# The last feed-forward of a decoder layer on one core: kept feature-major, with slots of 512 tokens

## The chip, the cores and the metric

The kernel runs on 1 core of one Trainium2 chip, as one program of six stages. The metric is the device time of one execution in microseconds. Engines are called as in the profile: PE (TensorE, with PEld for its weight loads), DVE (VectorE), ACT (ScalarE), POOL (GpSimd) and SP (the queue that issues DMAs).

## What is computed

A decoder layer over 4 sequences of 1024 tokens with 512 features: attention, a cross block with its own feed-forward, and last a quantised feed-forward, which is the only part that the change touches. Cut to that part:

```python
def act_quant(x):
    scale = 127.0 / clip(max(abs(x), axis=-1, keepdims=True), 1e-05)
    return clip(round(x * scale), -128, 127) / scale

x = layernorm(x)                         # 4 x 1024 x 512
h = einsum('bsd,hd->bsh', act_quant(x), weight_quant(w1))      # 512 -> 2048
h = depthwise_conv1d(h, conv_w, conv_b)  # 3 taps along the tokens, per feature
h = silu(h)
out = x_in + einsum('bsd,hd->bsh', act_quant(h), weight_quant(w2))   # 2048 -> 512
```

The convolution runs along the tokens of one feature. The quantisation of h needs, for each token, the largest absolute value over its 2048 features, and multiplies all of the token's features by one scale.

## The kernel before, in words

`quantised_ffn` (lines 2226 to 2550) is the last stage. The stage ahead has left the quantised x transposed in DRAM (`xq_parts`), with one scale factor per token (`x_units`); the weights w1 and w2 lie in DRAM as bf16 integers. Every engine has an instruction list of its own, written out by hand, and engines are tied by semaphores alone: `wait_ge` holds the engine's whole list until a count is reached. The order in each list is therefore what sets the order of the work.

For each of the 4 sequences (`body`) there are two halves.

- *Convolution half*, features on the partitions, 16 blocks (HB) of 128 features by 1024 tokens (T). PE makes a block in two PSUM banks of 512 tokens (L2424). DVE multiplies each bank by the token factors into `y` (`dequantise`, L2527). ACT makes the centre tap with the bias (L2465) and the right tap (L2468); DVE makes the centre tap of every fourth block instead (L2534) and adds the left tap for all (`add_left`, L2541); POOL adds the right tap (L2375); ACT applies SiLU into `h` (L2450), two blocks behind. y has two buffers, conv three.
- *Token half*, 8 tiles of 128 tokens. PE turns a tile of h, 16 transposes of 128 x 128 in fp32 (`turn_h`, L2394), so that tokens stand on the partitions. DVE takes the largest absolute value per token from PSUM (L2503) and makes the scale in five small steps (L2508 to L2497). ACT scales and adds 1.5 * 2^23, which rounds (L2456); POOL subtracts it again and writes bf16 (L2367). PE turns the tile back, 16 transposes in bf16 (`turn_hq`, L2403), ACT copies it out of PSUM (L2483), and PE multiplies by w2, 16 products (L2411). DVE scales the result and adds the residual (`finish`, L2517), SP stores it.

The token half of one sequence and the convolution half of the next use the same PSUM banks (`big`), so they follow one another.

SP's queue issues the loads (L2318, L2320, L2327, L2328, L2336) and the stores (L2324). At the start PE waits for both weights before its first product.

## Time and profile before

| | us |
|---|---|
| median of 3 runs (3616.22 to 3622.75) | 3618.28 |
| the profiled execution, its time | 3615.1 |
| the profiled execution, its span (first to last instruction) | 3613.4 |
| first issue of the last stage (SP L2318) | 3094.76 |
| first DVE pass of the last stage (L2527) | 3118.49 |

Busy over the whole span: PE 88%, PEld 64%, DVE 65%, ACT 51%, POOL 30%. These shares are means over six stages with different limits, and the last stage is about one seventh of the span. A line of the profile gives, for a group of equal instructions, how many there are (x64), the sum of their time, the mean of one in ns, and how long the engine stood idle just ahead of them and for whom. A timeline row gives start, length and, in brackets, the idle time ahead with its releaser. L numbers are lines of the kernel.

### The profile page before, as it was taken

Reading aid. Unit: us, or ns where it says so; the run is one execution under the profiler, and the core shown is the slowest. Engines: PE = TensorE matmul, PEld = TensorE weight load, DVE = VectorE, ACT = ScalarE, POOL = GpSimd, SP = SyncE. Lnnn points to the kernel's source line nnn. Section 1 sums busy time; section 2 is a strip of 40 time slices with the busy share of each in tenths; the row PEclk is TensorE's granted clock in tenths of the full one; section 3 lists DMA queues with packets and bytes.
Section 4 is the critical chain, followed back from the end, with each engine's and each line's share of the span. In section 5 each row is a group of like instructions: output and inputs, shape, how many; then the busy total and the mean of one; then the engine's idle time right before and its main releaser. Section 6 shows DMA issues by size and latency. Waiting matters only on the chain. (4 is left out here: it accounts for less than half of the span.)

```text
span 3613.4 us, 55879 instructions
## 1 busy us (share of the span) xinstructions
PE 3183.6 (88%) x19218; PEld 2307.8 (64%) x19218; DVE 2336.2 (65%) x4146; ACT 1842.0 (51%) x2979; POOL 1079.9 (30%) x829
## 2 busy tenths in 40 slices
PE   6998999999999999599996998599999998376687
PEld 5776666666666666377774777488878886143244
DVE  5563888888888888445644888444444445567766
ACT  3331888888888888322222222222222221467676
POOL 2343213112211311242322454211111110356555
PEclk9999999999999999799997999799999999688998
DMA  6775113212212221555536343321111101320111
GB/s 212 243 248 164 56 56 90 61 55 80 71 58 64 82 63 56 182 194 187 200 128 199 117 146 102 127 69 31 37 34 41 42 30 41 94 65 18 47 47 42
DMA packets 239599, 350.47 MB, mean 97 GB/s; under 512 B 31792, under 2 KB 129104, under 8 KB 239440
## 3 DMA queue, kind: packets, MB, share of 16 engines
q1 hardware_dynamic: 208784, 291.46, 25.2%
q0 software_dynamic: 8640, 31.77, 2.6%
q10 hardware_dynamic: 22016, 25.17, 2.0%
q8 instruction: 93, 1.52, 0.2%
q14 instruction: 66, 0.54, 0.1%
HBM read 210.68 MB, written 137.64 MB: 96 GB/s over the span
## 5 line engine op out<-in xcount | busy, mean ns | idle before, releaser
L863 DVE CUSTOM_DVE_ANT_0 attend_scores<-attend_scores,attend_bias_table 128x1024 f32<-128x1024 f32 x512 | 630.4, 1231 | 163.4 <-PE attend_scores L717 157.0
L790 ACT ACTIVATE attend_probs<-attend_scores,attend_neg_max 128x1024 f32<-128x1024 f32 x512 | 571.0, 1115 | 136.6 <-DVE attend_neg_max L863 126.7
L729 PE MATMUL attend_turned<-attend_ident,attend_probs 128*128 128x128 f32 x4096 | 556.5, 275 | 11.4 <-DVE attend_probsT L871 11.2
L729 PEld LDWEIGHTS attend_turned<-attend_ident,attend_probs 128*128 128x128 f32 x4096 | 471.9, 140 | 121.1 <-DVE attend_probsT L871 28.1
L717 PE MATMUL attend_scores<-attend_k_stack,attend_q_stack 96*128 96x512 f32 x1024 | 374.4, 447 | 14.4 <-DMA attend_q_stack<-qk_parts 9.7
L798 ACT COPY attend_probsT<-attend_turned 128x512 f32<-128x512 f32 x640 | 359.1, 583 | 24.8 <-PE attend_turned L729 23.1
L2207 DVE TENSOR_TENSOR cross_ffn_h_lo<-cross_ffn_hidden,cross_ffn_h_hi 128x512 fp32r<-128x512 f32 x128 | 96.5, 758 | 362.3 <-ACT cross_ffn_h_hi L2104 361.7
L744 PE MATMUL attend_out_acc<-attend_probsT,attend_v_in 128*32 128x256 f32 x4096 | 312.9, 389 | 0.7 <-DVE attend_out_full L881 0.7
L691 POOL TENSOR_TENSOR attend_out_parts<-attend_out_full,attend_out_parts 128x256 fp32r<-128x256 f32 x64 | 46.5, 726 | 855.5 <-ACT attend_out_parts L805 855.5
L871 DVE COPY attend_probsT<-attend_turned 128x512 f32<-128x512 f32 x384 | 263.3, 686 | 1.0 <-PE attend_turned L729 1.0
L717 PEld LDWEIGHTS attend_scores<-attend_k_stack,attend_q_stack 96*128 96x128 f32 x1024 | 153.9, 189 | 171.8 <-issue 169.2
L2101 ACT ACTIVATE cross_ffn_hidden<-cross_ffn_h_acc,cross_ffn_b_cols 128x512 f32<-128x512 f32 x128 | 88.1, 688 | 264.9 <-PE cross_ffn_h_acc L2018 248.8
L2424 PE MATMUL quantised_ffn_big<-quantised_ffn_xqT,quantised_ffn_w1T 128*128 128x512 bf16 x512 | 133.9, 415 | 100.4 <-DVE quantised_ffn_y L2527 67.4
L685 POOL TENSOR_TENSOR attend_bias_table<-attend_neg_distance,attend_slope_now 128x1920 f32<-128x1920 f32 x64 | 214.8, 3387 | 1.4
L2016 PE MATMUL cross_ffn_h_acc<-cross_ffn_aT_hi,cross_ffn_w_hi 128*128 128x512 f32 x512 | 203.4, 397 | 5.1 <-issue 5.1
L2029 PE MATMUL cross_ffn_out_acc<-cross_ffn_w_hi,cross_ffn_h_hi 128*128 128x512 f32 x512 | 206.4, 403 | 1.1 <-DVE cross_ffn_h_lo L2207 0.4
L2104 ACT CAST cross_ffn_h_hi<-cross_ffn_hidden 128x512 fp32r<-128x512 f32 x128 | 79.5, 621 | 247.6 <-PE cross_ffn_out_acc L2031 246.6
L2017 PE MATMUL cross_ffn_h_acc<-cross_ffn_aT_hi,cross_ffn_w_lo 128*128 128x512 f32 x512 | 202.8, 396 | 0.0
L2030 PE MATMUL cross_ffn_out_acc<-cross_ffn_w_lo,cross_ffn_h_hi 128*128 128x512 f32 x512 | 202.4, 395 | 0.0
L2031 PE MATMUL cross_ffn_out_acc<-cross_ffn_w_hi,cross_ffn_h_lo 128*128 128x512 f32 x512 | 202.2, 395 | 0.0
L2018 PE MATMUL cross_ffn_h_acc<-cross_ffn_aT_lo,cross_ffn_w_hi 128*128 128x512 f32 x512 | 202.0, 394 | 0.0
L2375 POOL TENSOR_TENSOR quantised_ffn_conv<-quantised_ffn_conv,quantised_ffn_right_tap 128x1024 f32<-128x1024 f32 x64 | 158.0, 2468 | 140.2 <-DVE quantised_ffn_conv L2541 135.9
(296 smaller groups left out, 6624.3 us busy)
## 6 DMA issues: line engine op xcount, KB each, us to landing
qk_parts<-qkv_qk_out SPq DMA_DIRECT2D x64, 512.0 KB, 3.2
attend_k_stack<-qk_parts SPq DMA_DIRECT2D x192, 128.0 KB, 2.5
attend_q_stack<-qk_parts SPq DMA_DIRECT2D x192, 128.0 KB, 2.7
qkv_wq_raw<-L_ffn_w POOLq DMA_DIRECT2D x16, 1024.0 KB, 7.7
o_parts<-attend_out_parts ACTq DMA_DIRECT2D x64, 256.0 KB, 2.5
mix_in_o_in<-o_parts SPq DMA_DIRECT2D x32, 512.0 KB, 6.7
qkv_x_in<-x SPq DMA_DIRECT2D x8, 1024.0 KB, 6.2
v_rows<-qkv_v_out SPq DMA_DIRECT2D x32, 256.0 KB, 3.4
```

The source lines that it names most:

```text
L685: pool.tensor_tensor(bias_table[:, h], neg_distance[:, :], slope_now[:, h:h + 1].to_broadcast([P, SPAN]), ALU.mult).then_inc(table_ready, 1)
L717: last = pe.matmul(scores[:, i % 2, k * HALF:(k + 1) * HALF], q_stack[:, h, queries], k_stack[:, h, k * HALF:(k + 1) * HALF], start=True, ...
L729: last = pe.transpose(turned[:, x, c], probs[:, i % 2, k * P:(k + 1) * P], ident[:, :])
L744: last = pe.matmul(out_acc[rows, 0:QG], v_in[:, c, rows], probsT[:, (qg - 1) % 2, c, h], start=(c == 0), stop=(c == TB - 1))
L790: act.activation(probs[:, i % 2], scores[:, i % 2], ACT.Exp, bias=neg_max[:, i % 4:i % 4 + 1], scale=-1.0, accum_out=den[:, qg % 2, j, h:h ...
L798: act.copy(probsT[:, qg % 2, x * HB:(x + 1) * HB, h, j * P:(j + 1) * P], turned[:, x]).then_inc(copied[x], 1)
L863: dve.tensor_tensor_reduce(scores[:, i % 2], scores[:, i % 2], bias_table[:, h, at:at + T], -1.0, BIG, ALU.add, ALU.min, neg_max[:, i % 4: ...
L871: dve.tensor_copy(probsT[:, qg % 2, HB:TB, h, j * P:(j + 1) * P], turned[:, 1]).then_inc(copied[1], 1)
L2016: pe.matmul(out, w1_hi[:, c, cols], aT_hi[:, c], start=c == 0, stop=False)
L2017: pe.matmul(out, w1_lo[:, c, cols], aT_hi[:, c], start=False, stop=False)
L2029: pe.matmul(out_acc[:, t], hi, w2_hi[:, j], start=j == 0, stop=False)
L2030: pe.matmul(out_acc[:, t], hi, w2_lo[:, j], start=False, stop=False)
```

## The change

The token half is gone. h stays with its features on the partitions, and the work is cut into slots of one block of 128 features by 512 tokens: 8 units (half a sequence each) of 16 blocks make 128 slots. All engines run one loop over slot numbers `s` to `END` = 169, and each step of a block stands a fixed lag behind the first: left tap 1, SiLU 2, maxima 3, scaling (POOL) 22, rounding (DVE) 23, product with w2 39.

- The largest value per token: DVE reduces four blocks at a time over blocks (`find_max`), then the four results, which leaves one value per partition and token; PE turns that (4 transposes), DVE reduces over the partitions' values and makes the scales (`scales`).
- The scales are spread over all partitions by a product of ones with a diagonal matrix of them (`spread_scale`), and ACT copies them into `scale_row`.
- POOL multiplies a block by `scale_row` (`scale_block`), DVE adds and subtracts 1.5 * 2^23 in one pass that writes bf16 (`round_block`). The result is directly the weight operand of the product with w2.
- Since a slot is half a sequence, the column beyond the half's edge is needed: `edge_products` computes two columns per block with 128 products of one column for each sequence, `find_edges` scales them, ACT copies one into `y` in each slot (`set_edge`).
- The centre tap is always ACT's. The second sequence's load is issued ahead of w2T. PE has 3 accumulators (`acc`) and 2 for the output.

The new lists (the removed functions are those printed above; `finish` only has other indices):

```diff
-    GW = 2 * D
-    CR = 3
+    CR, ACC = 3, 3
+    UNITS = 2 * B
+    SLOTS = UNITS * HB
+    TILES = N // P
+    SCALE_STEPS = 5
+    TURN_AT, SPREAD_AT, ROUND_AT = HB + 3, HB + 5, HB + 6
+    PRODUCT_AT = ROUND_AT + HB + 1
+    END = (UNITS - 1) * HB + PRODUCT_AT + HB + 2
...
+h = sb("h", [P, 2, HB, HALF])
+hqT = sb("hqT", [P, 2, HB, HALF], BF16)
...
+diag = sb("diag", [P, HT, P])
+scale_row = sb("scale_row", [P, 2, HALF])
+h_scaled = sb("h_scaled", [P, 2, HALF])
...
-big = ps("big", [P, 4, D])
-turned = ps("turned", [P, 2, GW], BF16)
-out_acc = ps("out_acc", [P, D])
+acc = ps("acc", [P, ACC, HALF])
+out_acc = ps("out_acc", [P, 2, D])
+max_turned = ps("max_turned", [P, HT, P])
+spread = ps("spread", [P, HALF])
...
+def block_at(s, lag):
+    return s - lag if 0 <= s - lag < SLOTS else None
+def half_at(s, lag):
+    u, f = divmod(s - lag, HB)
+    return u if f == 0 and 0 <= u < UNITS else None
+def product_at(s):
+    u, f = divmod(s - PRODUCT_AT, HB)
+    return (u * HT + f // 4, f % 4) if 0 <= u < UNITS else (None, None)
+def finish_at(s):
+    j, part = product_at(s - 1)
+    return j if part == 3 else None
...
         load_x(0)
         sp.dma_start(w1T[:, :, :], w1T_parts.rearrange("k p n -> p k n")).then_inc(w_loaded[0], 16)
+        load_x(1)
         sp.dma_start(w2T[:, :, :], w2T_parts.rearrange("f p n -> p f n")).then_inc(w_loaded[1], 16)
...
+        for s in range(END):
+            u, f = divmod(s, HB)
+            if f == 2 and u % 2 == 0 and 0 < u < UNITS - 2:
+                load_x(u // 2 + 1)
+            j, part = product_at(s)
+            if part == 0:
+                past(sp, out_done, j - 3)
+                sp.dma_start(x2_in[:, j % 4], tile_of(x2_rows, j)).then_inc(x2_loaded[j % 4], 16)
+            j = finish_at(s - 1)
+            if j is not None:
+                sp.wait_ge(out_done, j + 1)
+                sp.dma_start(tile_of(out_rows, j), out[:, j % 2]).then_inc(stored[j % 2], 16)
...
+        def add_right(i):
+            pool.wait_ge(right_ready, i + 1)
+            pool.wait_ge(left_added, i + 1)
+            pool.tensor_tensor(conv[:, i % CR], conv[:, i % CR], right_tap[:, i % 2], ALU.add).then_inc(right_added, 1)
+        def scale_block(i):
+            u, f = divmod(i, HB)
+            pool.wait_ge(scale_row_ready, u + 1)
+            past(pool, hq_ready, i - 1)
+            pool.tensor_tensor(h_scaled[:, i % 2], h[:, u % 2, f], scale_row[:, u % 2], ALU.mult).then_inc(h_scaled_ready, 1)
+        for s in range(END):
+            if s < SLOTS:
+                add_right(s)
+            i = block_at(s, ROUND_AT)
+            if i is not None:
+                scale_block(i)
...
+        def edge_products(b):
+            pe.wait_ge(xq_loaded[b % 2], (b // 2 + 1) * 16)
+            past(pe, scale_row_ready, 2 * b - 1)
+            for f in range(HB):
+                for k, col in ((0, P - 1), (1, 0)):
+                    for c in range(KB):
+                        last = pe.matmul(spread[:, 2 * f + k:2 * f + k + 1], w1T[:, c, f * P:(f + 1) * P],
+                                         xqT[:, b % 2, HT - 1 + k, c * P + col:c * P + col + 1], start=c == 0, stop=c == KB - 1)
+            last.then_inc(edges_ready, 1)
+        def block_product(i):
+            u, f = divmod(i, HB)
+            b, s = u // 2, u % 2
+            past(pe, y_ready, i - ACC + 1)
+            for c in range(KB):
+                last = pe.matmul(acc[:, i % ACC], w1T[:, c, f * P:(f + 1) * P], xqT[:, b % 2, s * HT:(s + 1) * HT, c * P:(c + 1) * P],
+                                 start=c == 0, stop=c == KB - 1)
+            last.then_inc(h_ready, 1)
...
+        def turn_max(u):
+            pe.wait_ge(col_max_ready, u + 1)
+            past(pe, scale_step, (u - 1) * SCALE_STEPS + 1)
+            for t in range(HT):
+                last = pe.transpose(max_turned[:, t], col_max[:, t * P:(t + 1) * P], ident[:, :])
+            last.then_inc(max_turned_ready, 1)
+        def spread_scale(u):
+            pe.wait_ge(diag_ready, u + 1)
+            pe.wait_ge(edges_done, min((u + 1) // 2 + 1, B))
+            past(pe, scale_row_ready, u)
+            pe.matmul(spread[:, :], ones[:, :], diag[:, :, :].rearrange("p t n -> p (t n)"), start=True, stop=True)\
+              .then_inc(spread_ready, 1)
...
+        def w2_product(j, part):
+            u, t = divmod(j, HT)
+            if part == 0:
+                past(pe, out_done, j - 1)
                 if t == 0:
+                    pe.wait_ge(hq_ready, (u + 1) * HB)
+            for f in range(4 * part, 4 * part + 4):
+                last = pe.matmul(out_acc[:, j % 2], hqT[:, u % 2, f, t * P:(t + 1) * P], w2T[:, f], start=f == 0, stop=f == HB - 1)
+            if part == 3:
+                last.then_inc(out_ready, 1)
...
+        edge_products(0)
         pe.wait_ge(w_loaded[1], 16)
+        for s in range(END):
+            if s < SLOTS:
+                block_product(s)
+            j, part = product_at(s)
+            if j is not None:
+                w2_product(j, part)
+            u = half_at(s, TURN_AT)
+            if u is not None:
+                turn_max(u)
+            u = half_at(s, SPREAD_AT)
+            if u is not None:
+                spread_scale(u)
+            if s % (2 * HB) == HB + 8 and s // (2 * HB) + 1 < B:
+                edge_products(s // (2 * HB) + 1)
...
+            past(act, h_scaled_ready, i - 2 * HB + 1)
+            past(act, maxed, (u - 2) * 4 + f // 4 + 1)
+            act.activation(h[:, u % 2, f], conv[:, i % CR], ACT.Silu).then_inc(silu_done, 1)
+        def set_edge(i):
+            u, f = divmod(i, HB)
+            s = u % 2
+            act.wait_ge(edges_done, u // 2 + 1)
+            past(act, left_added, i - 1)
+            past(act, right_ready, i - 1)
+            edge = slice(HALF + 1, HALF + 2) if s == 0 else slice(0, 1)
+            act.copy(y[:, s, i % 2, edge], edges[:, u // 2 % 2, f, 1 - s:2 - s]).then_inc(y_edged, 1)
+        def taps_of(i):
+            u, f = divmod(i, HB)
+            s = u % 2
+            act.wait_ge(y_ready, i + 1)
+            past(act, silu_done, i - CR + 1)
+            act.activation(conv[:, i % CR], y[:, s, i % 2, 1:HALF + 1], ACT.Identity, bias=conv_bias[:, f:f + 1],
+                           scale=taps[:, f, 1:2]).then_inc(centre_ready, 1)
+            past(act, right_added, i - 1)
+            act.wait_ge(y_edged, i + 1)
+            act.activation(right_tap[:, i % 2], y[:, s, i % 2, 2:HALF + 2], ACT.Identity, scale=taps[:, f, 2:3])\
+                .then_inc(right_ready, 1)
+        for s in range(END):
+            if s < SLOTS:
+                set_edge(s)
+                taps_of(s)
+            i = block_at(s, 2)
+            if i is not None:
+                silu(i)
+            u = half_at(s, SPREAD_AT)
+            if u is not None:
+                act.wait_ge(spread_ready, u + 1)
+                past(act, h_scaled_ready, (u - 1) * HB)
+                act.copy(scale_row[:, u % 2], spread[:, :]).then_inc(scale_row_ready, 1)
...
+        def find_edges(b):
+            dve.wait_ge(edges_ready, b + 1)
+            dve.wait_ge(unit_loaded[b % 2], (b // 2 + 1) * 16)
+            past(dve, y_edged, 2 * (b - 1) * HB)
+            dve.tensor_tensor(edges[:, b % 2], spread[:, 0:2 * HB].rearrange("p (f k) -> p f k", k=2),
+                              unit_row[:, b % 2, HALF - 1:HALF + 1].unsqueeze(1).to_broadcast([P, HB, 2]), ALU.mult)\
+                .then_inc(edges_done, 1)
...
+        def dequantise(i):
+            u, f = divmod(i, HB)
+            b, s = u // 2, u % 2
+            past(dve, centre_ready, i - 1)
             past(dve, right_ready, i - 1)
             past(dve, left_added, i - 1)
+            dve.wait_ge(h_ready, i + 1)
+            dve.wait_ge(unit_loaded[b % 2], (b // 2 + 1) * 16)
+            dve.tensor_tensor(y[:, s, i % 2, 1:HALF + 1], acc[:, i % ACC], unit_row[:, b % 2, s * HALF:(s + 1) * HALF], ALU.mult)\
+                .then_inc(y_ready, 1)
...
+        def add_left(i):
+            u, f = divmod(i, HB)
+            dve.wait_ge(y_ready, i + 1)
+            dve.wait_ge(y_edged, i + 1)
+            dve.wait_ge(centre_ready, i + 1)
+            dve.scalar_tensor_tensor(out=conv[:, i % CR], in0=y[:, u % 2, i % 2, 0:HALF], scalar=taps[:, f, 0:1], in1=conv[:, i % CR],
                                      op0=ALU.mult, op1=ALU.add).then_inc(left_added, 1)
...
+        def find_max(i):
+            u, f = divmod(i, HB)
+            if f % 4 == 3:
+                dve.wait_ge(silu_done, i + 1)
+                past(dve, col_max_ready, u)
+                dve.tensor_reduce(group_max[:, f // 4], h[:, u % 2, f - 3:f + 1].rearrange("p f t -> p t f"), AX.X, ALU.max,
+                                  apply_absolute_value=True).then_inc(maxed, 1)
+            if f == HB - 1:
+                dve.wait_ge(maxed, (u + 1) * 4)
+                past(dve, max_turned_ready, u)
+                dve.tensor_reduce(col_max[:, :], group_max[:, :, :].rearrange("p g t -> p t g"), AX.X, ALU.max).then_inc(col_max_ready, 1)
+        def scales(u):
+            base = u * SCALE_STEPS
+            dve.wait_ge(max_turned_ready, u + 1)
+            past(dve, diag_ready, u)
+            dve.tensor_reduce(h_max[:, :], max_turned[:, :, :], AX.X, ALU.max).then_inc(scale_step, 1)
+            dve.wait_ge(scale_step, base + 1)
+            dve.tensor_scalar(h_max[:, :], h_max[:, :], FLOOR, None, ALU.max).then_inc(scale_step, 1)
+            dve.wait_ge(scale_step, base + 2)
+            dve.reciprocal(h_inverse[:, :], h_max[:, :]).then_inc(scale_step, 1)
+            past(dve, out_done, (u - 2) * HT)
+            dve.tensor_scalar(h_unit[:, u % 3], h_max[:, :], w_mean[:, 1:2], 1.0 / LIMIT, ALU.mult, ALU.mult).then_inc(scale_step, 1)
+            dve.wait_ge(scale_step, base + 4)
+            dve.tensor_scalar(h_scale[:, :], h_inverse[:, :], LIMIT, None, ALU.mult).then_inc(scale_step, 1)
+            dve.wait_ge(scale_step, base + 5)
+            past(dve, spread_ready, u)
+            dve.tensor_tensor(diag[:, :, :], ident[:, :].unsqueeze(1).to_broadcast([P, HT, P]),
+                              h_scale[:, :].unsqueeze(2).to_broadcast([P, HT, P]), ALU.mult).then_inc(diag_ready, 1)
+        def round_block(i):
+            u, f = divmod(i, HB)
+            dve.wait_ge(h_scaled_ready, i + 1)
+            if f == 0:
+                past(dve, out_ready, (u - 1) * HT)
+            dve.tensor_scalar(hqT[:, u % 2, f], h_scaled[:, i % 2], ROUND, -ROUND, ALU.add, ALU.add).then_inc(hq_ready, 1)
...
+        find_edges(0)
+        for s in range(END):
+            if s < SLOTS:
+                dequantise(s)
+            i = block_at(s, 1)
+            if i is not None:
+                add_left(i)
+            i = block_at(s, ROUND_AT + 1)
+            if i is not None:
+                round_block(i)
+            i = block_at(s, 3)
+            if i is not None:
+                find_max(i)
+            u = half_at(s, TURN_AT + 1)
+            if u is not None:
+                scales(u)
+            j = finish_at(s)
+            if j is not None:
+                finish(j)
+            if s % (2 * HB) == HB + 9 and s // (2 * HB) + 1 < B:
+                find_edges(s // (2 * HB) + 1)
```

## Rows read from the trace of the kernel before

**Rows 1.** Windows view of the last stage: length; busy PE, PEld, DVE, ACT, POOL; granted clock.

```profile
3242.00:3300.00 58.00, 36.64 (x141) 14.68 (x138) 54.99 (x53) 45.02 (x42) 35.28 (x15) 0.88 0.12 41
3300.00:3364.00 64.00, 50.95 (x372) 33.97 (x373) 33.79 (x80) 39.18 (x51) 36.47 (x34) 0.90 0.17 55
```

**Rows 2.** Timeline of the convolution half (start us, length us, engine, line, operation).

```profile
3246.12 1.28 DVE L2541 SCALAR_TENSOR_TENSOR quantised_ffn_conv<-quantised_ffn_y,quantised_ffn_taps,quantised_ffn_conv 128x1024 f32<-128x1024 f32 x1
...
3247.54 2.38 POOL L2375 TENSOR_TENSOR quantised_ffn_conv<-quantised_ffn_conv,quantised_ffn_right_tap 128x1024 f32<-128x1024 f32 x1 [13.33 <-DVE quantised_ffn_conv L2541]
3247.60 1.29 DVE L2527 TENSOR_TENSOR quantised_ffn_y<-quantised_ffn_big,quantised_ffn_unit_row 128x512 f32<-128x512 f32 x2 [0.20 <-DVE quantised_ffn_conv L2541]
...
3248.80 2.19 DVE L2541 SCALAR_TENSOR_TENSOR quantised_ffn_conv<-quantised_ffn_y,quantised_ffn_taps,quantised_ffn_conv 128x1024 f32<-128x1024 f32 x1
...
3251.14 2.35 POOL L2375 TENSOR_TENSOR quantised_ffn_conv<-quantised_ffn_conv,quantised_ffn_right_tap 128x1024 f32<-128x1024 f32 x1 [1.23 <-DVE quantised_ffn_conv L2541]
...
3253.59 1.15 ACT L2468 ACTIVATE quantised_ffn_right_tap<-quantised_ffn_y,quantised_ffn_taps 128x1024 f32<-128x1024 f32 x1 [1.44 <-POOL quantised_ffn_conv L2375]
```

**Rows 3.** Who waited for whom in the last stage: us in total, times, longest.

```profile
POOL quantised_ffn_conv L2375 <- DVE quantised_ffn_conv L2541: 135.9, 61, 25.9
```

**Rows 4.** One tile, the convolution's: durations min/median/max in ns.

```profile
L2541 DVE SCALAR_TENSOR_TENSOR quantised_ffn_conv<-quantised_ffn_y,quantised_ffn_taps,quantised_ffn_conv x64: 1276/2181/3178, 3123.4 to 3544.6; 128x1024 f32<-128x1024 f32 x64
L2375 POOL TENSOR_TENSOR quantised_ffn_conv<-quantised_ffn_conv,quantised_ffn_right_tap x64: 2337/2363/2806, 3124.8 to 3548.0; 128x1024 f32<-128x1024 f32 x64
```

**Rows 5.** Timeline of the token half, one token tile.

```profile
3200.99 1.92 PE L2394 MATMUL quantised_ffn_big<-quantised_ffn_ident,quantised_ffn_h 128*128 128x128 f32 x16
...
3204.15 0.16 DVE L2508 TENSOR_REDUCE quantised_ffn_h_max<-quantised_ffn_bank_max 128x1 f32<-128x4 f32 x1
...
3204.73 0.15 DVE L2497 TENSOR_SCALAR quantised_ffn_h_scale<-quantised_ffn_h_inverse 128x1 f32<-128x1 f32 x1
...
3206.20 1.06 PE L2403 MATMUL quantised_ffn_turned<-quantised_ffn_ident,quantised_ffn_hq 128*128 128x128 bf16 x16
```

**Rows 6.** One tile each, instructions of 512 elements: durations min/median/max in ns.

```profile
L1125 POOL TENSOR_TENSOR mix_in_emb_bo<-mix_in_emb,mix_in_bias_o x32: 1263/1287/1297, 1522.6 to 1860.7; 128x512 f32<-128x512 f32 x32
...
L2196 DVE TENSOR_SCALAR cross_ffn_xq<-cross_ffn_xn x32: 426/427/1406, 2441.8 to 3082.5; 128x512 bf16<-128x512 f32 x32
...
L2160 DVE SCALAR_TENSOR_TENSOR cross_ffn_z<-cross_ffn_z,cross_ffn_rstd,cross_ffn_x_in x32: 742/746/748, 2428.8 to 3065.1; 128x512 f32<-128x512 f32 x32
```

**Rows 7.** Groups of the last stage: line, operation, shapes, count, busy us, mean ns.

```profile
L2527 DVE TENSOR_TENSOR quantised_ffn_y<-quantised_ffn_big,quantised_ffn_unit_row 128x512 f32<-128x512 f32 x128 | 83.1, 685 | 48.2 <-PE quantised_ffn_big L2424 38.8 <-DVE quantised_ffn_conv L2541 6.1 <-ACT quantised_ffn_right_tap L2468 2.4
L2503 DVE TENSOR_REDUCE quantised_ffn_bank_max<-quantised_ffn_big 128x1 f32<-128x512 f32 x128 | 81.7, 685 | 37.6 <-PE quantised_ffn_big L2394 37.4
...
L2517 DVE SCALAR_TENSOR_TENSOR quantised_ffn_out<-quantised_ffn_out_acc,quantised_ffn_h_unit,quantised_ffn_x_in 128x512 f32<-128x512 f32 x32 | 24.0, 751 | 81.9 <-PE quantised_ffn_out_acc L2411 81.9
```

**Rows 8.** One tile, a reduction of 1024 elements in SBUF, min/median/max ns.

```profile
L1337 DVE TENSOR_REDUCE mix_in_neg_max<-mix_in_kT x16: 1199/1203/1222, 1598.1 to 1893.7; 128x1 f32<-128x1024 f32 x16
```

**Rows 9.** Timeline of the start of the last stage.

```profile
3095.82 0.43 SPq L2327 DMA_DIRECT2D quantised_ffn_w1T<-w1T_parts  x1
...
3097.53 12.77 SPq L2318 DMA_DIRECT2D quantised_ffn_xqT<-xq_parts  x1
...
3118.49 0.69 DVE L2527 TENSOR_TENSOR quantised_ffn_y<-quantised_ffn_big,quantised_ffn_unit_row 128x512 f32<-128x512 f32 x1 [35.57 <-PE quantised_ffn_big L2424]
```

**Rows 10.** DMA issues of the last stage: KB each, median us to landing.

```profile
quantised_ffn_w1T<-w1T_parts SPq DMA_DIRECT2D x1, 2048.0 KB, 14.4
quantised_ffn_w2T<-w2T_parts SPq DMA_DIRECT2D x1, 2048.0 KB, 19.9
```

**Rows 11.** Group of ScalarE: a 512-wide pass over SBUF.

```profile
L1274 ACT ACTIVATE mix_in_expq<-mix_in_q_full 128x512 f32<-128x512 f32 x32 | 20.2, 630 | 53.8 <-DVE mix_in_q_full L1342 42.1 <-DMA expq_rows<-mix_in_expq 11.6
```

**Rows 12.** Timeline of the stage's end.

```profile
3605.78 3.61 PE L2411 MATMUL quantised_ffn_out_acc<-quantised_ffn_w2T,quantised_ffn_hqT 128*128 128x512 bf16 x16 [0.75 <-ACT quantised_ffn_hqT L2483]
3609.53 0.75 DVE L2517 SCALAR_TENSOR_TENSOR quantised_ffn_out<-quantised_ffn_out_acc,quantised_ffn_h_unit,quantised_ffn_x_in 128x512 f32<-128x512 f32 x1 [4.50 <-PE quantised_ffn_out_acc L2411]
```

More of the change, by code:

```diff
@@ L2397, in turn_hq @@
-                def turn_hq(i, t):
-                    for s in range(2):
-                        pe.wait_ge(hq_ready, i * 4 + 2 * (s + 1))
-                        past(pe, hqT_ready, (i - 1) * 2 + s + 1)
-                        for k in range(8):
-                            at = (s * 8 + k) * P
-                            last = pe.transpose(turned[:, s, k * P:(k + 1) * P], hq[:, t % 2, at:at + P], ident16[:, :])
-                        last.then_inc(hq_turned, 1)
-                def w2_product(i, t):
-                    past(pe, out_done, i)
-                    for f in range(HB):
-                        if f % 8 == 0:
-                            pe.wait_ge(hqT_ready, i * 2 + f // 8 + 1)
-                        last = pe.matmul(out_acc[:, :], hqT[:, t % 2, f * P:(f + 1) * P], w2T[:, f], start=f == 0, stop=f == HB - 1)
-                    last.then_inc(out_ready, 1)
@@ new lines, in _ @@
+                pe.wait_ge(ident_step, 2)
+                def edge_products(b):
[7 more added lines that the diff above has]
+                    last.then_inc(edges_ready, 1)
@@ L2443, in _, with silu @@
                 act.wait_ge(const_step, 6)
[L2445 to L2446 removed]
+                def silu(i):
+                    u, f = divmod(i, HB)
                     act.wait_ge(right_added, i + 1)
[L2448 to L2457 removed]
@@ L2544, in body @@
-                def body(b, more):
-                    dve.wait_ge(unit_loaded[b % 2], (b // 2 + 1) * 16)
-                    for f in range(HB):
-                        dequantise(b, f)
-                        if f:
-                            add_left(b, f - 1)
-                        if by_dve(f):
-                            centre(b, f)
-                    add_left(b, HB - 1)
-                    scale_h(b * TB, 0)
-                    for t in range(TB):
-                        if t + 1 < TB:
-                            scale_h(b * TB + t + 1, t + 1)
-                        if t:
-                            finish(b, t - 1)
-                    finish(b, TB - 1)
@@ new lines, in round_block, with finish @@
+                def round_block(i):
+                    u, f = divmod(i, HB)
+                    dve.wait_ge(h_scaled_ready, i + 1)
+                    if f == 0:
+                        past(dve, out_ready, (u - 1) * HT)
+                    dve.tensor_scalar(hqT[:, u % 2, f], h_scaled[:, i % 2], ROUND, -ROUND, ALU.add, ALU.add).then_inc(hq_ready, 1)
+                def finish(j):
+                    u, t = divmod(j, HT)
+                    dve.wait_ge(x2_loaded[j % 4], (j // 4 + 1) * 16)
+                    past(dve, stored[j % 2], j // 2 * 16)
+                    dve.wait_ge(out_ready, j + 1)
+                    dve.scalar_tensor_tensor(out=out[:, j % 2], in0=out_acc[:, j % 2], scalar=h_unit[:, u % 3, t:t + 1], in1=x2_in[:, j % 4],
+                                             op0=ALU.mult, op1=ALU.add).then_inc(out_done, 1)
```

218 lines of the change are left out of this document (26 added, 192 removed).

## The prediction

> **What bounds the kernel now.** Only the last stage changes, so I read the last stage: first its busy times by stretch, then its timeline. A sequence takes two stretches of about 60 us [rows 1]. In the convolution half VectorE (DVE) is busy 54.99 of 58 us while GpSimd (POOL) shows 35.28; in the token half no engine is above 51 of 64 us. The reader should see in the timeline [rows 2] what the 54.99 is made of: the left-tap add of 1024 elements takes 1.28 us with POOL idle, but 2.19 us when it starts beside POOL's right-tap add, and it then ends at 3250.99, 1.07 us after POOL's end (3249.92). POOL starts again at 3251.14. The block period is thus POOL 2.36 + 1.07 + 0.15, a closed ring of two engines: 135.9 us of POOL's idle time ends on that very DVE line [rows 3]. The tile view says it is the normal case, median 2181 against a least of 1276 ns [rows 4].
>
> The token half is a ring too: h turned (16 in 1.92 us), five small scale steps (3204.15 to 3204.88), rounded, turned back (16 in 1.06 us) [rows 5].
>
> **What the change removes.** All 512 + 512 transposes of h and hq, ScalarE's scaled passes and copies, POOL's 128 subtractions. The stage now runs from 3118.5 (first DVE pass) to 3613.4: 495 us, 3.87 us for each of 128 slots of 128 features by 512 tokens. That is the figure to beat. (A difference below 0.2%, 7 us, couldn't be told from none.)
>
> **What the new order makes of a slot.** I follow the waits in the code, engine by engine, in a slot where all is in flight.
> - DVE, slot s+1: dequantise(s+1), add_left(s), round_block(s-22), then maxima, finish.
> - POOL, slot s: add_right(s), then scale_block(s-22).
> - add_right(s) waits for add_left(s), which stands in DVE's slot s+1. round_block(s-22), next in DVE's queue, waits for scale_block(s-22), which stands behind add_right(s) in POOL's queue.
>
> So after add_left DVE stands still for two whole POOL passes; behind it in its queue are the maxima, the finish, the next dequantise and the next add_left, and POOL waits for the last of these. Nothing of POOL's runs beside anything of DVE's. The slot is a sum:
> - signal DVE to POOL 0.14 (3247.40 to 3247.54 [rows 2]);
> - two POOL passes of 512 fp32 elements with both inputs full: 1.287 each, less 0.04 for back to back, 2.53 [rows 6]. Half a 1024 pass would be 1.18 each [rows 4];
> - signal POOL to the next engine 0.10 (3253.49 to 3253.59 [rows 2]);
> - round_block 0.43 [rows 6], add_left 0.75 (same shape and form, 746 ns [rows 6]), dequantise 0.69 [rows 7]; the two that are followed by another DVE pass count 0.08 less each (two L2527 passes take 1.29, not 1.37): 1.71.
>
> Together 4.48 us. Both passes are present in DVE's slots 23 to 128, 106 of them: 475 us.
>
> On top, in DVE's queue and so in the same ring:
> - Maxima. Each group maximum and each column maximum reads 4 x 512 elements with the four 2 KB apart. From 685 ns for 512 [rows 7] and 1203 for 1024 [rows 8] one more element costs 1.01 ns, so 2048 cost 2.25, 2.2 in a queue. 26 + 6 fall into these slots: 70 us. No row shows a read with such steps; the bounds are 2.2, and 4.4 if each element cost what POOL's does (2.1 ns, from 1287 and 2363 [rows 4, 6]). I take 2.2, because the kind, the engine and the memory are those of rows 7 and 8.
> - 22 finishes of 0.751 [rows 7], 0.67 in a queue: 15 us.
> - 6 times the scales: a 512 maximum 0.69, four small steps 0.6 (five take 0.73 [rows 5]), the diagonal 0.69 as any 512-wide product of two tensors [rows 7], two gaps: 2.1, so 13 us. Three edge products with unit: 1 us.
>
> Sum of the 106 slots: **574 us**, 5.4 each.
>
> **The other stretches.**
> - *Start.* The weights w1T are issued at 3095.82 [rows 9] and land 14.4 later [rows 10]: 3110.2. Then come 128 one-column products. The nearest row is the bf16 transposes, 0.066 us each [rows 5]: 8.5 us, or 17 at half that rate. Beside it w2T, which landed 19.9 after an issue right behind w1T's, near 3116 [rows 10], now stands behind a load whose issue took SP's queue 12.77 us [rows 9]. The first dequantise came at 3118.49 [rows 9]; now 3121 to 3129, I take 3125.5, 7 later.
> - *Slots 0 to 22*, no rounding. POOL's pass 1.29, the rest of add_left after it 0.55 (0.20 was hidden: 1.28 - 1.07 [rows 2]), signal 0.14: 1.98 us. ScalarE's three passes take 0.63 each [rows 11], 0.55 in a queue, with the edge's one element (taken as 0.2) 1.85, and fit into it. 18 such slots make 36; 5 with a group maximum, which hides POOL's pass, 3.55 each, 18; a column maximum and one scales, 4.3. Sum 58 us.
> - *DVE's slots 129 to 150*, scaling and rounding alone: 1.29 + 0.43 + 0.14, as a ring of two buffers in which rounding has to follow POOL's next pass: 1.86, times 22: 41 us. The last scales and finishes lie beside.
> - *Tail.* The last half's 4 token tiles, 64 products at 3.61/16 [rows 12]: 14 us; from the last product's end (3609.4) to 3613.4: 4 us. Sum 18.
>
> TensorE costs nothing elsewhere: 8 products in a slot are 1.8 us, and stand 3 blocks ahead. Even at double time (3.6) they fit into 5.4, so without that cover nothing is lost but the tail's 14. The later edge products (8.5 to 17 us) lie under three slots of lead, 16 us. The spread product and its copy are two slots ahead of their user. SP's loads and stores hang on finish and lie 3 tiles ahead.
>
> End: 3125.5 + 58 + 574 + 41 + 18 = 3816.5 against 3613.4, **203 us later**. The profiled execution itself took 3615.1 us, 1.7 around its span and 3 below the median 3618.3; I add the difference to the median: **3821 us**, 5.6% slower.
>
> **A rule of the Trainium skill, weighed.** The trace shows a DVE pass with two SBUF inputs standing still until POOL's ends [rows 2]. The Trainium skill, SBUF — State Buffer, section "Who interferes with whom", says the same of any such pass and of 2-port modes: whoever comes second is blocked fully. By it the new ring is no longer than summed, since DVE already waits while POOL works. The same page of the Trainium skill, section "SBUF: two separate sides", says that reads which leave a 16-byte line each time pay a penalty, of no stated size for DVE. No row here shows it. It speaks against the maxima, as the first rival does, whose numbers are the rows'.
>
> **The rivals.**
> 1. *The strided maxima cost double* (4.4 us each). 32 + 5 + 1 + 2 of them are all in the ring: +2.2 x 40 = 88, so 3909. For: no row shows steps of 2 KB at DVE's rate. (The Trainium skill, SBUF — State Buffer, section "SBUF: two separate sides", names such a penalty.) Against: rows 7 and 8 show about 1 ns per element from PSUM as from SBUF, so the engine and not the memory seems to set it. Chance 0.24.
> 2. *TensorE falls to its 1.2 GHz level.* It rests 3.6 of 5.4 us in a slot, where before it had 0.88 to 0.90 granted at 37 busy of 58 [rows 1]. Hidden except in the tail: +14, 3835, inside the forecast's range. Chance 0.05.
> 3. *The ring isn't closed, the shared port binds*: if POOL came a slot ahead, DVE wouldn't wait, but its add_left and round_block still exclude POOL's passes: 2.53 + 0.55 + 0.43 + 0.28 = 3.79, the maxima beside it: 402 instead of 574, so 3649. Against: add_right's wait for add_left ties POOL to DVE's slot. Chance 0.05.
> 4. *Faster*: scale_block's result lies ready each time round_block comes, and neither blocks the other. Its place is round_block's wait, 2.77 us in my sum (signals and POOL). Then a slot is DVE's own 1.71 less the last 0.08, 1.63, 173 us + 99 = 272, so 3519. It decides from 3.5 us a slot (574 - 203 over 106), that is where no more than 0.85 of the 2.77 is left. For: h_scaled has two buffers, so its ring would let POOL be a block ahead. Against: POOL is held by add_left before it comes to that buffer. Chance 0.05.
>
> **How the numbers follow.** Forecast 0.61. Its low end: POOL passes at 1.18 (-23), add_left at half of 1.28 (-12), the start 4 earlier (-4), gaps 0.05 less a slot (-5): 3777; with a little for DVE passes that overlap more, 3770. Its high end, start +4 and some 0.1 a slot of waits between own steps, 3840. Adding rival 1 gives the range 3770 to 3912; rivals 3 and 4 stay out (0.10). Slower 0.61 + 0.24 + 0.05 + 0.04 of rival 3 = 0.94, less 0.01 for what I don't see: 0.93; same 0.02; faster 0.05.
>
> **What would show it.** After: POOL's L-line for scale_block starts right after add_right; round_block's idle time ends on POOL's h_scaled, about 2.7 us in each of 106 slots, 290 us in all; POOL's idle ends on add_left; slot period 4.5 us, over 7 with a maximum; maxima 2.2 us; TensorE's busy share down to a third. Wrong if DVE and POOL show passes side by side in mid-stage, if round_block hardly waits, or if the stage is under 495 us. The maxima's duration alone tells rival 1.

## The result, and the profile after

The changed kernel takes **3862.85 us** (median of 4 runs, 3860.37 to 3863.8) against 3618.14 for the kernel before: ratio **1.0673 [1.0655, 1.0692]**, 245 us slower where 203 were forecast. The profiled execution's span is 3858.8 us, against the 3816.5 of the sum. The last stage now takes 735 us from its first dequantise to its end, where it took 495.

Windows view of the kernel after, cut close to the prediction's stretches (columns as in [rows 1], and behind the clock the DMA share and GB/s):

```profile
3123.80:3192.00 68.20, 38.20 (x208) 14.23 (x207) 58.32 (x57) 47.49 (x92) 28.00 (x22) 0.73 0.00 1
3192.00:3792.00 600.00, 283.37 (x1085) 103.36 (x1099) 318.08 (x410) 216.29 (x426) 262.25 (x210) 0.70 0.08 25
3792.00:3838.00 46.00, 24.30 (x84) 9.55 (x84) 32.79 (x37) 1.22 (x2) 30.68 (x24) 0.72 0.21 69
3838.00:3858.80 20.80, 16.26 (x63) 6.75 (x64) 3.93 (x6) 0.00 (x0) 0.00 (x0) 0.83 0.32 102
```

In the 600 us of the middle DVE's and POOL's busy times together are 580: two engines that work by turns. PE's granted clock, 0.88 to 0.90 in [rows 1], is down to 0.70, so a good part of the time it has its 1.2 GHz level.

Waits of the kernel after, over the last stage:

```profile
ACT quantised_ffn_conv L2464 <- DVE quantised_ffn_y L2503: 410.8, 114, 9.5
POOL quantised_ffn_conv L2355 <- DVE quantised_ffn_conv L2511: 403.1, 128, 27.8
DVE quantised_ffn_hqT L2550 <- POOL quantised_ffn_h_scaled L2361: 293.9, 115, 3.0
```

The second line is that of [rows 3], 135.9 us in 61 times before. The third is new and closes the ring. The first says that ScalarE has become idle for more than half of the stage.

DVE and POOL in the timeline of the kernel after, one plain slot and one with a group maximum:

```profile
3405.18 0.68 DVE L2503 TENSOR_TENSOR quantised_ffn_y<-quantised_ffn_acc,quantised_ffn_unit_row 128x512 f32<-128x512 f32 x1
3405.78 0.74 DVE L2511 SCALAR_TENSOR_TENSOR quantised_ffn_conv<-quantised_ffn_y,quantised_ffn_taps,quantised_ffn_conv 128x512 f32<-128x512 f32 x1
...
3406.67 1.27 POOL L2355 TENSOR_TENSOR quantised_ffn_conv<-quantised_ffn_conv,quantised_ffn_right_tap 128x512 f32<-128x512 f32 x1 [1.86 <-DVE quantised_ffn_conv L2511]
...
3407.90 1.29 POOL L2361 TENSOR_TENSOR quantised_ffn_h_scaled<-quantised_ffn_h,quantised_ffn_scale_row 128x512 f32<-128x512 f32 x1
...
3409.22 0.43 DVE L2550 TENSOR_SCALAR quantised_ffn_hqT<-quantised_ffn_h_scaled 128x512 bf16<-128x512 f32 x1 [2.70 <-POOL quantised_ffn_h_scaled L2361]
...
3410.16 0.74 DVE L2511 SCALAR_TENSOR_TENSOR quantised_ffn_conv<-quantised_ffn_y,quantised_ffn_taps,quantised_ffn_conv 128x512 f32<-128x512 f32 x1
...
3413.57 0.43 DVE L2550 TENSOR_SCALAR quantised_ffn_hqT<-quantised_ffn_h_scaled 128x512 bf16<-128x512 f32 x1 [2.67 <-POOL quantised_ffn_h_scaled L2361]
3413.91 3.61 DVE L2520 TENSOR_REDUCE quantised_ffn_group_max<-quantised_ffn_h 128x512 f32<-128x2048 f32 x1
3417.44 0.68 DVE L2503 TENSOR_TENSOR quantised_ffn_y<-quantised_ffn_acc,quantised_ffn_unit_row 128x512 f32<-128x512 f32 x1
3418.04 0.74 DVE L2511 SCALAR_TENSOR_TENSOR quantised_ffn_conv<-quantised_ffn_y,quantised_ffn_taps,quantised_ffn_conv 128x512 f32<-128x512 f32 x1
```

From one add_left (L2511) to the next: 4.38 us in the plain slot (3405.78 to 3410.16), 7.88 with the maximum (to 3418.04). While POOL works DVE stands still, and the other way round. The maximum takes 3.61 us, where [rows 7] and [rows 8] had led me to 2.2.

The start and the end, timeline of the kernel after:

```profile
3110.90 3.56 PE L2382 MATMUL quantised_ffn_spread<-quantised_ffn_xqT,quantised_ffn_w1T 128*128 128x1 bf16 x128 [26.41 <-DMA quantised_ffn_w1T<-w1T_parts]
...
3121.89 3.17 PE L2391 MATMUL quantised_ffn_acc<-quantised_ffn_xqT,quantised_ffn_w1T 128*128 128x512 bf16 x7 [7.43 <-DMA quantised_ffn_w2T<-w2T_parts]
...
3123.82 0.69 DVE L2503 TENSOR_TENSOR quantised_ffn_y<-quantised_ffn_acc,quantised_ffn_unit_row 128x512 f32<-128x512 f32 x1 [8.95 <-PE quantised_ffn_acc L2391]
...
3838.41 4.00 PE L2417 MATMUL quantised_ffn_out_acc<-quantised_ffn_w2T,quantised_ffn_hqT 128*128 128x512 bf16 x9 [4.71 <-DVE quantised_ffn_hqT L2550]
```

PE stands 7.43 us for w2T, of which no product has need for another 39 slots. The last products begin at the 1.2 GHz level: 0.44 us each for the first nine, where [rows 12] has 0.23.

### The profile page after: what moved, and what is told of

Read it like the earlier page. It is cut to its first block and busy times, and to the rows that moved or that the text cites. A ratio compares the mean times of both kernels' runs of the same rounds, so it can differ in the third digit from the quotient of the medians.

```text
span 3858.8 us, 55765 instructions
## 1 busy us (share of the span) xinstructions
PE 3202.1 (83%) x18735; PEld 2252.1 (58%) x18754; DVE 2394.5 (62%) x4126; ACT 1768.9 (46%) x3131; POOL 1113.7 (29%) x892
## 5 line engine op out<-in xcount | busy, mean ns | idle before, releaser
L2391 PE MATMUL quantised_ffn_acc<-quantised_ffn_xqT,quantised_ffn_w1T 128*128 128x512 bf16 x512 | 186.8, 509 | 172.1 <-DVE quantised_ffn_y L2503 164.4
L2464 ACT ACTIVATE quantised_ffn_conv<-quantised_ffn_y,quantised_ffn_conv_bias,quantised_ffn_taps 128x512 f32<-128x512 f32 x128 | 104.2, 814 | 411.0 <-DVE quantised_ffn_y L2503 410.8
L2355 POOL TENSOR_TENSOR quantised_ffn_conv<-quantised_ffn_conv,quantised_ffn_right_tap 128x512 f32<-128x512 f32 x128 | 162.4, 1269 | 403.1 <-DVE quantised_ffn_conv L2511 403.1
L2550 DVE TENSOR_SCALAR quantised_ffn_hqT<-quantised_ffn_h_scaled 128x512 bf16<-128x512 f32 x128 | 64.8, 511 | 293.9 <-POOL quantised_ffn_h_scaled L2361 293.9
L2391 PEld LDWEIGHTS quantised_ffn_acc<-quantised_ffn_xqT,quantised_ffn_w1T 128*128 128x128 bf16 x512 | 55.2, 120 | 295.5 <-DVE quantised_ffn_y L2503 216.3
L2417 PE MATMUL quantised_ffn_out_acc<-quantised_ffn_w2T,quantised_ffn_hqT 128*128 128x512 bf16 x493 | 165.9, 479 | 46.6 <-DVE quantised_ffn_hqT L2550 26.3
```

The lines of the kernel that those rows point to most:

```text
L2355: pool.tensor_tensor(conv[:, i % CR], conv[:, i % CR], right_tap[:, i % 2], ALU.add).then_inc(right_added, 1)
L2391: last = pe.matmul(acc[:, i % ACC], w1T[:, c, f * P:(f + 1) * P], xqT[:, b % 2, s * HT:(s + 1) * HT, c * P:(c + 1) * P], start=c == 0, sto ...
L2417: last = pe.matmul(out_acc[:, j % 2], hqT[:, u % 2, f, t * P:(t + 1) * P], w2T[:, f], start=f == 0, stop=f == HB - 1)
```

## The experiments

My theory: the ring through round_block's wait costs some 2.7 us a slot, and the maxima cost 1.4 us each for the steps of their reads. Rivals: the shared port alone would hold the stage; the maxima are slow for another reason (the size, the 512 outputs, a neighbour engine).

**1. Rounding one slot later.** It moves nothing but the place where DVE waits, and with it the product with w2 by a slot.

```diff
-    PRODUCT_AT = ROUND_AT + HB + 1
+    PRODUCT_AT = ROUND_AT + HB + 2
-            i = block_at(s, ROUND_AT + 1)
+            i = block_at(s, ROUND_AT + 2)
```

> Rounding stands one slot later in DVE's list (lag 24, product lag 40), everything else as changed. Ring theory: the wait of round_block for two POOL passes (2.77 us in each of 106 slots) goes, and the shared port binds next: POOL 2.5, the rest of add_left 0.55, rounding 0.43, a signal 0.14, so 3.6 us a slot, 5.3 in a slot with a group maximum, 4.05 in the mean, about 175 us less: 3688 us. Rival 'that idle time costs nothing': 3863 as before. Rival 'the port doesn't matter': DVE's own work, 3.0 us a slot: about 3576.

Measured: 3719.4, ratio 1.0279 [1.0262, 1.0296]. By the ratios 0.0394 of 3617 are won back, 143 us, with not one instruction less. Two waits in the changed kernel, the same two in this one, then DVE and POOL in its timeline:

```profile
DVE quantised_ffn_hqT L2550 <- POOL quantised_ffn_h_scaled L2361: 293.9, 115, 3.0
DVE quantised_ffn_y L2503 <- PE quantised_ffn_acc L2391: 14.4, 4, 9.0
```

```profile
DVE quantised_ffn_hqT L2550 <- POOL quantised_ffn_h_scaled L2361: 60.7, 54, 1.2
DVE quantised_ffn_y L2503 <- PE quantised_ffn_acc L2391: 33.1, 15, 9.1
```

```profile
3406.54 1.32 POOL L2355 TENSOR_TENSOR quantised_ffn_conv<-quantised_ffn_conv,quantised_ffn_right_tap 128x512 f32<-128x512 f32 x1 [3.81 <-DVE quantised_ffn_conv L2511]
...
3407.25 1.17 DVE L2511 SCALAR_TENSOR_TENSOR quantised_ffn_conv<-quantised_ffn_y,quantised_ffn_taps,quantised_ffn_conv 128x512 f32<-128x512 f32 x1
...
3407.83 1.73 POOL L2361 TENSOR_TENSOR quantised_ffn_h_scaled<-quantised_ffn_h,quantised_ffn_scale_row 128x512 f32<-128x512 f32 x1
```

The ring is shown: the wait fell from 293.9 to 60.7 us. What is left is that the passes of DVE and POOL exclude each other (the shared port of the prediction). DVE's add_left stands until POOL's first pass ends (3407.86) and then runs its last 0.56 us; POOL's next pass, started at 3407.83, takes 1.73 in place of 1.28. So not all of the 228 us of waiting that went from slots 23 to 127 is won. There the mean rounding now takes 0.86 us (0.43 in the changed kernel) and the mean add_left 0.93 (0.74), and with the small passes that is 69 us; DVE's waits for PE's next product, of which the changed kernel has none in these slots, are 19 more. Four slots with one maximum take 16.06 us in this trace (3400.11 to 3416.17, between two roundings), 4.02 a slot, which is what I had expected (4.05). The 31 us that are missing lie outside such groups: over slots 23 to 127 a slot takes 4.37, since 4.05 had no place for the column maxima, the scales and the waits for PE.

**2. Maxima read in the order of the memory.** Same sizes, each output over four neighbouring elements, so the maxima are taken over neighbouring tokens and not over blocks. The diff shows the group maxima; the column maxima are changed in the same way.

```diff
-    h[:, u % 2, f - 3:f + 1].rearrange("p f t -> p t f")
+    h[:, u % 2, f - 3:f + 1].rearrange("p f t -> p (f t)").rearrange("p (t f) -> p t f", f=4)
...
```

> The 40 maxima read the same 2048 elements in the order of memory instead of four elements 2 KB apart (they then take maxima over neighbouring tokens, which is not the quantity wanted; everything else stays). Theory that the step costs 1.37 us each and that all stand in the ring: 2.25 us each, 40 x 1.37 = 55 us less: 3808 us. Rival 'small groups of four cost it, not the step': 3.6 us each and 3863. Rival 'the maxima are hidden': 2.25 us each and 3863.

Measured: 3807.32, ratio 1.0526 [1.0509, 1.0544]; 53 us less than the changed kernel by the ratios. The tile view of its maxima:

```profile
L2520 DVE TENSOR_REDUCE quantised_ffn_group_max<-quantised_ffn_h x32: 2271/2278/2286, 3139.8 to 3750.4; 128x512 f32<-128x2048 f32 x32
```

2278 in place of 3611 ns (the same view of the kernel after): 1.33 us in each of 40 maxima are 53. The steps are the cause, and all of it lies in the ring.

**3. Both edits together.**

> Both edits together. Ring theory: with the ring open the maxima run beside POOL's passes, so the 1.37 us are worth less than alone: a slot with a maximum 4.0, the mean 3.7, about 35 us below the first run: 3655 us. Rival 'costs simply add up': 55 below the first run.

Measured: 3661.97, ratio 1.0124 [1.0107, 1.0141], 57 us below the first experiment. The two costs add up in full, as the rival had it; I had thought that with the ring open part of the maxima would find cover. DVE's wait for the scaling is the same 50.5 us in slots 23 to 127 of both runs, so a shorter maximum shortens DVE's own path and nothing waits in its place.

**4. Which steps cost.** Reductions behind DVE's last pass, one after the other, of 2048 elements to 512 outputs with steps of 4, 8, 16 bytes inside an output, then with 2 KB; last, 1024 elements in pairs, 4 bytes and 2 KB apart. One run, read for the durations alone; each reduction stands in it three times.

> The changed kernel with DVE reductions of up to 2048 elements behind its last pass, read for their durations only. If leaving a 16-byte line each time is what costs: four with step 1 take 2.25 us, step 2 (two to a line) nearly that, step 4 and step 8 3.6 as the 2 KB step; 16 inputs to an output the same by the step. If it is the number of outputs: 128 outputs of 16 are cheaper than 512 of 4 at any step.

The view of that one line, one row for each (left out: steps of 32 bytes, and two with 16 elements to an output):

```profile
L2600 DVE TENSOR_REDUCE quantised_ffn_probe<-quantised_ffn_h x1: 2286/2286/2286, 3857.3 to 3857.3; 128x512 f32<-128x2048 f32 x1
L2600 DVE TENSOR_REDUCE quantised_ffn_probe<-quantised_ffn_h x1: 2286/2286/2286, 3859.7 to 3859.7; 128x512 f32<-128x2048 f32 x1
L2600 DVE TENSOR_REDUCE quantised_ffn_probe<-quantised_ffn_h x1: 3743/3743/3743, 3862.0 to 3862.0; 128x512 f32<-128x2048 f32 x1
...
L2600 DVE TENSOR_REDUCE quantised_ffn_probe<-quantised_ffn_h x1: 3619/3619/3619, 3869.6 to 3869.6; 128x512 f32<-128x2048 f32 x1
...
L2600 DVE TENSOR_REDUCE quantised_ffn_probe<-quantised_ffn_h x1: 1220/1220/1220, 3879.2 to 3879.2; 128x512 f32<-128x1024 f32 x1
L2600 DVE TENSOR_REDUCE quantised_ffn_probe<-quantised_ffn_h x1: 1230/1230/1230, 3880.5 to 3880.5; 128x512 f32<-128x1024 f32 x1
```

The number of outputs isn't it (the shape is the same), nor is a neighbour (PE, ACT and POOL have no instruction here). Nor is it the four elements to an output: 16 to an output take 2286 ns in the order of the memory and 3578 with far steps. Steps of 8 bytes are free, 16 cost 1.64 times, 32 bytes (3811 ns) and 2 KB about the same. And pairs that lie 2 KB apart are free as well, while fours are not.

**5. POOL scales first.** The other way to open the ring, two calls in POOL's list exchanged:

```diff
         for s in range(END):
-            if s < SLOTS:
-                add_right(s)
             i = block_at(s, ROUND_AT)
             if i is not None:
                 scale_block(i)
+            if s < SLOTS:
+                add_right(s)
```

> Only the order of two calls in POOL's list is exchanged: scale_block(s-22) ahead of add_right(s). All lags stay. Ring theory: scale_block no longer stands behind a pass that waits for DVE's slot, so round_block finds it done or under way; 4.0 us a slot as in the run with the rounding a slot later, 3710 to 3730 us. Rival 'only a longer lag helps': 3863 as before.

Measured: 3688.84, ratio 1.0189 [1.0172, 1.0206]: 175 us won back by the order of two calls, 33 more than by the first experiment. From its waits:

```profile
DVE quantised_ffn_hqT L2550 <- POOL quantised_ffn_h_scaled L2361: 39.6, 34, 3.0
POOL quantised_ffn_conv L2355 <- DVE quantised_ffn_conv L2511: 209.7, 103, 28.1
```

scale_block has what it needs since many slots; first in the list it fills the time in which POOL would wait for add_left. Against experiment 1 over slots 23 to 127, of its 32 us less 22 are a shorter wait of the rounding (50.5 to 28.2) and 9 are DVE's waits for PE (18.6 to 9.4); why PE keeps up better with this order I haven't shown.

**6. Pairs in the layout.** h and group_max hold two blocks side by side, so that the true maxima read pairs of 8 bytes.

```diff
-h = sb("h", [P, 2, HB, HALF])
+h = sb("h", [P, 2, HB // 2, HALF, 2])
...
-    h[:, u % 2, f - 3:f + 1].rearrange("p f t -> p t f"), AX.X
+    h[:, u % 2, f // 2 - 1:f // 2 + 1].rearrange("p g t k -> p t g k"), AX.XY
```

> h and the group maxima lie in pairs of blocks (step of 8 bytes from token to token), and each maximum of four reads two pairs. Theory from the durations of the last run, that two elements to a 16-byte line are read at full rate: 2.29 us a maximum, 3808 us as with the flat reading, plus what SiLU's writing and POOL's reading with a step of 8 bytes cost, each microsecond of which counts in the ring 128 times. Rival 'it needs neighbouring addresses all through': 3.6 to 3.8 us a maximum and 3863.

Measured: 3813.73, ratio 1.0537 [1.052, 1.0555]. In its tile view the maxima have the length of experiment 2:

```profile
L2520 DVE TENSOR_REDUCE quantised_ffn_group_max<-quantised_ffn_h x32: 2272/2279/2286, 3142.0 to 3755.3; 128x512 f32<-128x2048 f32 x32
```

So 49 of the 53 us are had with the maxima taken over the blocks, as they must be. Of the few that are missing some 2 can go to POOL's scaling, which reads with 8-byte steps and stands in the ring 106 times (median 1290 ns, 1270 in the changed kernel); the rest is less than the interval. SiLU, which writes with such steps, takes 653 ns (613), but ScalarE isn't in the ring.

**7. The wait for w2T at its first product.**

```diff
-        pe.wait_ge(w_loaded[1], 16)
...
+                if s == PRODUCT_AT:
+                    pe.wait_ge(w_loaded[1], 16)
```

> TensorE waits for w2T at its first product with w2 (slot 39) and no longer ahead of slot 0. The first block product starts at about 3114.5 instead of 3121.9, so 7 us less: 3856 us. Rival 'the start is covered by other loads' (token factors): 3863.

Measured: 3855.19, ratio 1.0651 [1.0633, 1.0669]: 8 us below the changed kernel, by the medians as by the ratios. The intervals of the two ratios overlap, so the traces have to say it: from the first edge product to the first dequantise it is 5.32 us here (3115.37 to 3120.69) and 12.92 in the changed kernel (3110.90 to 3123.82).

**8. A version that is faster.** ScalarE, idle in half of each slot, takes the rounding in two passes (add, then subtract); h_scaled has four buffers; with 6 and 7. What each part gives alone wasn't run.

```diff
+def raise_block(i):
+    act.wait_ge(h_scaled_ready, i + 1)
+    act.activation(h_scaled[:, i % 4], h_scaled[:, i % 4], ACT.Identity, bias=round_up[:, :]).then_inc(rounded_up, 1)
+def round_block(i):
...
+    act.activation(hqT[:, u % 2, f], h_scaled[:, i % 4], ACT.Identity, bias=round_down[:, :]).then_inc(hq_ready, 1)
```

> ScalarE rounds (two passes of 0.55 us in a queue, lags 24 and 25), product lag 41, pairs of blocks for the maxima, the late wait for w2T. DVE no longer waits for POOL's scaling at all, and one pass less wants the shared port. Ring theory: POOL's two passes 2.5 and the rest of add_left 0.56 bind, 3.1 us a slot, 3.25 with the slots that hold a maximum; the last 22 scaling slots 1.3 each. From the run with both edits, 3662: 67 less in mid-stage, 12 at its end, 7 at the start: about 3580 us, faster than the kernel before. Rival 'ScalarE binds' (3.2 us of passes a slot, and its waits): 3.6 a slot, about 3620.

Measured: 3603.48, ratio 0.9955 [0.9939, 0.9972]. A slot of its ScalarE in the timeline:

```profile
3400.41 0.20 ACT L2463 COPY quantised_ffn_y<-quantised_ffn_edges 128x1 f32<-128x1 f32 x1
3400.50 0.82 ACT L2470 ACTIVATE quantised_ffn_conv<-quantised_ffn_y,quantised_ffn_conv_bias,quantised_ffn_taps 128x512 f32<-128x512 f32 x1
3401.22 0.72 ACT L2474 ACTIVATE quantised_ffn_right_tap<-quantised_ffn_y,quantised_ffn_taps 128x512 f32<-128x512 f32 x1
3401.83 0.68 ACT L2454 ACTIVATE quantised_ffn_h<-quantised_ffn_conv 128x512 f32<-128x512 f32 x1
3402.39 0.71 ACT L2479 ACTIVATE quantised_ffn_h_scaled<-quantised_ffn_h_scaled,quantised_ffn_round_up 128x512 f32<-128x512 f32 x1
3403.00 0.72 ACT L2486 ACTIVATE quantised_ffn_hqT<-quantised_ffn_h_scaled,quantised_ffn_round_down 128x512 bf16<-128x512 f32 x1
3403.61 0.19 ACT L2463 COPY quantised_ffn_y<-quantised_ffn_edges 128x1 f32<-128x1 f32 x1
```

3.2 us, back to back in this slot: ScalarE is nearly full (333 of 361 us over slots 23 to 127), as the rival had it. A slot there takes 3.47 us, between my 3.25 and the rival's 3.6, and the time lies between the two as well. PE's list still waited for ScalarE (out_acc on hqT, 40.8 us in 8 times).

**9. The product two slots later.** The ninth is the eighth with `PRODUCT_AT = ROUND_AT + HB + 5` for `+ 3`.

> The last version with the product lag at 43 instead of 41. Theory: in the last version TensorE waited once a unit for ScalarE's last rounded block (40.8 us in 8 waits) with the next block product behind it in its list, which stopped DVE too; two slots of lag take these stops out, about 4 us for each of 6 or 7 units: 3575 to 3580 us. Rival 'ScalarE, filled to 3.2 us a slot, binds anyway and made up for the stops': 3600.

Measured: **3594.31, ratio 0.9929 [0.9911, 0.9947]**, the fastest of all, 25 us (0.7%) below the kernel before, though 14 to 19 above what I expected and nearer the rival's 3600. Over slots 23 to 127 DVE's waits for PE fell from 39.7 to 16.6 us, and those for ScalarE's centre tap rose from 28.4 to 35.7. Its windows view, in mid-stage, beside that of the changed kernel:

```profile
3400.00:3500.00 100.00, 65.63 (x275) 27.29 (x271) 81.24 (x85) 95.29 (x180) 79.36 (x60) 0.81 0.13 43
```

```profile
3400.00:3500.00 100.00, 47.48 (x144) 16.97 (x148) 53.14 (x70) 36.76 (x72) 43.52 (x35) 0.77 0.13 42
```

ScalarE, the fourth busy time, is at 95 of 100 us, where it had 37; DVE and POOL together come to 161, which two engines that take turns can't reach.

**10. Every fourth block rounded by DVE again**, on top of the ninth.

```diff
+def by_dve(i):
+    return i % 4 == 1
```

> As the run beside it, and DVE rounds every fourth block in one pass. If ScalarE's 3.2 us a slot is what binds, it falls to 2.9 and POOL's 3.1 binds: another 10 us less. Rival 'the shared port binds': the pass of DVE's that excludes POOL costs 0.1 us a slot more: no gain or 10 us more.

Measured: 3604.51, ratio 0.9954 [0.9936, 0.9971], 10 us slower than the ninth. ScalarE got room (86 busy of 100 us, from 3400 to 3500), but waits for DVE's dequantise 68.5 us in 44 times, against 33.0 in 24 in the ninth. DVE shows 84 and POOL 81 there, and one of DVE's roundings takes 1.21 us in the mean over slots 23 to 127: a pass given to DVE costs more than it frees. So ScalarE alone wasn't the bound of the ninth.

## Why the prediction was right, step by step

Right in sign and mechanism; each stretch against the trace, in us:

| stretch | forecast | measured |
|---|---|---|
| first dequantise at | 3125.5 | 3123.8 |
| slots 0 to 22 | 58 | 69.0 |
| the 106 slots | 574 | 602.6 |
| DVE's slots 129 to 150 | 41 | 42.9 |
| tail | 18 | 20.5 |

The slots end with DVE's roundings at 3795.4 and 3838.3. The differences add up to the 42 us between the spans. The forecast itself reached to 3840 only; 3863 lies within the stated range because the first rival was taken into it. Without the steps in the maxima the kernel takes 3807 (experiment 2), beside the 3821 of the sum.

- **The ring**, forecast at 4.48 us, is 4.38: the wait 2.67 to 2.70 where I had 2.77, the rest DVE's own. Over 106 slots 11 us less. The 290 us of waiting in these slots were 283.5 (293.9 with the slots behind them), and experiments 1 and 5 show that they hang on the order in the lists alone.
- **The maxima were the term that was mis-sized.** "I take 2.2, because the kind, the engine and the memory are those of rows 7 and 8": kind, engine and memory were right, and the order of the addresses, which neither row had, was what counted. They cost 3.5 in the ring (7.88 less 4.38): 42 us more in 32 of them; with the 11 of the ring that is the stretch's 29 but for 2. Experiments 2 and 6 put all 40 at 53 and 49. The first rival had the mechanism and too high a size (4.4).
- The steps of 8 and of 16 bytes (2286 and 3743 ns) agree with the Trainium skill, Advanced Engine Details and Errata, section "Memory Cachelines", by which SBUF has lines of 16 bytes and full speed needs at least two hits on a line. That section of the Trainium skill also has every access on another line pay; the pairs 2 KB apart are such accesses, two lines in turn, and cost 1230 against 1220 ns. There the measurement decides.
- **Slots 0 to 22**: 6 maxima at 1.3 more are 8 us. The other 4 go against "TensorE costs nothing elsewhere": PE's list holds turn_max and spread_scale, which wait for DVE, ahead of the next block's products. In the kernel after:

```profile
3179.99 0.69 DVE L2503 TENSOR_TENSOR quantised_ffn_y<-quantised_ffn_acc,quantised_ffn_unit_row 128x512 f32<-128x512 f32 x1 [1.85 <-PE quantised_ffn_acc L2391]
...
3187.84 0.69 DVE L2503 TENSOR_TENSOR quantised_ffn_y<-quantised_ffn_acc,quantised_ffn_unit_row 128x512 f32<-128x512 f32 x1 [2.54 <-PE quantised_ffn_acc L2391]
```

  Later slots are twice as long, and the wait doesn't come again in this kernel. Where the slots are shorter it does: 18.6 us over slots 23 to 127 in experiment 1.
- **The start** was right for a wrong reason in part: the edge products take 0.028 us each (3.56 for 128), not 0.066; the wait for w2T, which the forecast had only as a possible delay beside them, sets the time, and experiment 7 gives its 8 us back.
- **The clock** of the second rival fell indeed (0.70), against the 0.05 I gave it; as that rival had said it cost nothing in slots 23 to 127, where DVE never waits for PE; in the tail it cost 2 us and not 14, since only the first nine products ran at the lower level. TensorE's busy share, which was to go down to a third, is 0.47 (283 of 600 us): at the lower level a product takes longer.
- The third rival (port and no ring) is what experiment 1 made of the kernel: 4.37 us a slot and 3719, where it had 3.79 and 3649. It had the maxima beside POOL's passes; experiment 3 shows that they find no cover. The fourth asked that no more than 0.85 us of the wait be left in a slot; 2.67 were (283.5 in 106).

## What to carry to other kernels

Before a pass is put behind another engine's wait, write both lists side by side: where each holds the other's producer behind its own wait, the engines work by turns and their times add up; here exchanging two calls gave back 175 us of 245. A layout that spares transposes is to be priced with the addresses that its reductions then read: in these reductions on DVE two partners side by side cost nothing extra, and four single words from four places cost 1.6 times. And ask which engine is left idle by what was removed: here ScalarE was, and with the rounding given to it, pairs in the layout, the late wait for w2T and the later product, the new version came out 0.7% faster than the old.
